# Moving the high parts of the key, value and output weights from ScalarE to GpSimd in the first pass of a gated cross-attention kernel

## The chip, the cores and the metric

The kernel runs on one core of a Trainium2 chip. The metric is the device time of one execution in microseconds (us), the median of several runs. The engines are named as the profile names them: PE is TensorE (matmuls), PEld its weight loads, DVE is VectorE, ACT is ScalarE, POOL is GpSimd and SP is SyncE, whose queue issues all the DMAs here.

## The reference

The block adds a gated cross-attention and then a gated quantised linear layer to `x` (32 sequences of 64 tokens, width 512). There are 32 query heads and 8 key/value heads of width 128.

```python
Q = (q @ Wq.T).reshape(b, s, HKV, exp, DK)      # q = layernorm(x)
K = (k @ Wk.T).reshape(b, s, HKV, DK)           # k = v = ctx
V = (v @ Wv.T).reshape(b, s, HKV, DV)
scores = jnp.einsum('bqhed,bkhd->bheqk', Q, K) * scale
scores = jnp.where(causal, scores, jnp.finfo(scores.dtype).min)
probs = jax.nn.softmax(scores, axis=-1)
attn = jnp.einsum('bheqk,bkhd->bqhed', probs, V)
attn @ Wd.T
...
x = x + jnp.tanh(g_xattn[0]) * _L0_xattn_ref(_layernorm(x), ctx, ctx, Wq, Wk, Wv, Wd)
x = x + jnp.tanh(g_ffn[0]) * _L0_ffn_ref(_layernorm(x), qweight, weight_scale, weight_zero_point, bias)
```

## The kernel before

**Numbers.** All is float32 in the reference. The kernel multiplies in float16: each operand is scaled by a power of two and split into a high part (the float16 value) and a low part (what is left, in float16), and a product is made of three matmuls: high by high, high by low, low by high (`PASSES`).

**Work.** The 2048 tokens are four blocks of 512, the heads are eight groups (one key/value head with its four query heads). A step `n` of the main loop is one group `g = n % 8` in one block `tb = n // 8`, so there are 32 steps. In step `n` PE makes the scores, the transposed probabilities, the products with the values (`av`) and, with the group's output weights `wd`, the four output tiles (`y_unit`, tile `py`), and between them, one step ahead, the queries, keys and values of step `m = n + 1` (tile `pa`). `y_unit(n, 0)` begins some 21 us into a step, and from there to the step's end nearly all of PE's work is `y_unit`.

**Weights.** The first eight steps (`tb == 0`) are the first pass. There the raw float32 weights of each group come from HBM and are scaled and split: `wq` by ACT (high part) and DVE (low part); `wk`, `wv` (one piece of 128x512 each per group) and `wd` (four pieces of 128x512) by ACT (high part, `split_wk`, `split_wv`, `split_wd` of ACT) and POOL (low part). For the low part POOL runs two instructions on a piece, `weight_lo`: `raw = raw * scale` in place (TENSOR_SCALAR, L430), then `lo = raw - high` (TENSOR_TENSOR, L432). The finished parts are written to HBM (`keep_qkv`, `keep_d`) and in later passes read back ready (`back_qkv`, `back_d`).

**Order.** Each engine has one queue, written by hand as a Python loop, and engines wait for each other by counting semaphores. In step `g` of the first pass POOL has: (in step 0 ahead of the rest, `wk(1)` and `wv(1)`), the twelve small instructions of `ln_rstd` where a layer norm falls due (step 6), the four pieces of `wd(g)`, the low parts of a normed block (`ln_lo`), two chunks of the next block's context (`ctx_lo`, steps 5 and 6), and `wk(g+2)`, `wv(g+2)` (steps 0 to 5). `wd` has a single buffer: `wd(g)` may be written only after the last `y_unit` of step `g-1` (`y_mm`) and after the copy to HBM of `wd(g-1)` (`d_kept`). The other weights have two buffers, by `g % 2`. The scale factors `w_mul` come from sums of squares (ACT), a small matmul (PE) and small DVE instructions (`weight_scale`), those for group `g+2` in step `g` just ahead of `y_unit(g, 0)`, after which PE waits for `wd_hi` and `wd_lo` (four counts per group).

**ACT's queue** in a step of the first pass, in short: `q_part 0`, `exp 0`, two pieces of `wd`, `q_part 1`, `p_part 0`, `exp 1`, two pieces of `wd`, `q_part 2`, squares of `wq(g+2)`, `p_part 1`, `q_part 3`, squares, `p_transposed 0`, squares of `wk` and `wv`, `k_part`, `p_transposed 1`, the `av` parts, `v_part`, `wq(g+2)`, `wk(g+2)`, `wv(g+2)`, squares of `wd`.

Of the kernel before, what the change touches and what calls it, by code (L numbers as in the profile page):

```python
# [52 lines left out]
def build(nc, x, ctxT, wqT, wkT, wvT, wdT, g_x, g_f, qw, w_scale, w_zero, bias, out):  # L53
    with ExitStack() as stack:
# [91 lines left out]
        q_kept, k_kept, v_kept, d_kept = sem("q_kept"), sem("k_kept"), sem("v_kept"), sem("d_kept")  # L146
# [111 lines left out]
        def _(sp):  # L258
# [25 lines left out]
            def keep_qkv(g):  # L284
# [120 lines left out]
        def _(pool):  # L405
# [117 lines left out]
        def _(act):  # L523
# [56 lines left out]
            def split_wk(g):  # L580
                act.wait_ge(w_mul_ok, scale_count(g, 1))
                wait(act, k_kept, 16 * (g - 1))
                act.wait_ge(wk_hi, g)
                act.activation(wk[:, g % 2, HI, :, :], raw_k[:, g % 2, :, :], ACT.Copy,
                               scale=w_mul[:, g, 1:2]).then_inc(wk_hi, 1)

            def split_wv(g):
                wait(act, v_kept, 16 * (g - 1))
# [857 lines left out]
```

## Time and profile before

| | |
|---|---|
| time, median of 3 runs | 1093.32 us (1093.08 to 1093.55) |
| profiled execution, its own time | 1090.95 us |
| its span, first to last instruction | 1089.2 us |
| busy: PE, DVE, ACT, POOL | 1033.6, 718.2, 489.3, 239.3 us |
| mean granted TensorE clock | 0.989 of full |

The span is what the trace covers; the profiled run's own time is 1.75 us longer, for what lies around it. A matmul's end is modelled in the trace, so PE's busy share tells that it is nearly always at work, not that each moment is full speed.

### The profile page before, as it was taken

Reading aid. Unit: us, or ns where it says so; the run is one execution under the profiler, and the core shown is the slowest. Engines: PE = TensorE matmul, PEld = TensorE weight load, DVE = VectorE, ACT = ScalarE, POOL = GpSimd, SP = SyncE. Lnnn points to the kernel's source line nnn. Section 1 sums busy time; section 2 is a strip of 40 time slices with the busy share of each in tenths; the row PEclk is TensorE's granted clock in tenths of the full one; section 3 lists DMA queues with packets and bytes.
Section 4 is the critical chain, followed back from the end, with each engine's and each line's share of the span. In section 5 each row is a group of like instructions: output and inputs, shape, how many; then the busy total and the mean of one; then the engine's idle time right before and its main releaser. Section 6 shows DMA issues by size and latency. Waiting matters only on the chain.

```text
span 1089.2 us, 20137 instructions
## 1 busy us (share of the span) xinstructions
PE 1033.6 (95%) x8000; PEld 582.6 (53%) x8000; DVE 718.2 (66%) x1347; ACT 489.3 (45%) x937; POOL 239.3 (22%) x242
## 2 busy tenths in 40 slices
PE   5899999999999999999999999999999999999974
PEld 3455554555555555555555555555555555555532
DVE  6856777677578566666665576755567566655567
ACT  5767675676534243353435334244434432333322
POOL 1545565466504100110004010110001300000012
PEclk9999999999999999999999999999999999999997
DMA  7647645435345133323332433332223233331101
GB/s 270 224 159 256 214 158 171 157 97 175 110 162 191 51 127 116 114 101 117 116 117 59 153 139 116 117 117 89 70 95 117 98 116 117 116 117 59 52 27 58
DMA packets 64250, 137.08 MB, mean 126 GB/s; under 512 B 5408, under 2 KB 38176, under 8 KB 53536
## 3 DMA queue, kind: packets, MB, share of 16 engines
q1 hardware_dynamic: 64160, 135.81, 36.4%
q8 instruction: 65, 1.06, 0.4%
q14 instruction: 25, 0.20, 0.1%
HBM read 93.85 MB, written 25.17 MB: 109 GB/s over the span
## 4 chain that ended last, share of the span: by engine, by line
PE 81%; DVE 8%; ACT 5%; issue 3%; POOL 0%; DVEq 0%; ACTq 0%; POOLq 0%
PE pa L1138 36%; PE py L1138 30%; PE av L1245 5%; PE ps L1212 3%; PE py L1295 3%; PE pp L1228 2%; PE av L1280 1%; DVE sc L846 1%; DVE row_max L850 1%; DVE sc L852 1%; ACT junk L542 1%; ACT junk L552 1%; DVE sc L863 1%; ACT pT L641 1%; DVE q L806 1%
## 5 line engine op out<-in xcount | busy, mean ns | idle before, releaser
L1138 PE MATMUL pa<-xT,wq 128*128 128x512 f16 x1536 | 347.1, 380 | 7.2 <-DVE q L806 4.6
L1138 PE MATMUL py<-wd,att 128*128 128x512 f16 x1536 | 349.8, 380 | 1.4 <-DVE att L876 1.3
L1138 PEld LDWEIGHTS pa<-xT,wq 128*128 128x128 f16 x1536 | 144.1, 98 | 179.6 <-issue 20.2
L1138 PEld LDWEIGHTS py<-wd,att 128*128 128x128 f16 x1536 | 148.9, 98 | 164.1 <-issue 4.0
L885 DVE SCALAR_TENSOR_TENSOR xacc<-py,f_y,xacc 128x512 f32<-128x512 f32 x128 | 96.0, 750 | 145.3 <-PE py L1138 145.3
L603 ACT ACTIVATE q<-pa 128x512 f16<-128x512 f32 x128 | 75.8, 592 | 235.2 <-PE pa L1138 235.1
L648 ACT ACTIVATE att<-av 128x256 f16<-128x256 f32 x256 | 80.9, 385 | 158.2 <-PE av L1245 157.8
L876 DVE SCALAR_TENSOR_TENSOR att<-av,att 128x256 f16<-128x256 f32 x256 | 93.6, 418 | 70.0 <-ACT att L648 70.0
L806 DVE SCALAR_TENSOR_TENSOR q<-pa,q 128x512 f16<-128x512 f32 x128 | 87.6, 685 | 22.6 <-ACT q L603 22.6
L1138 PE MATMUL pa<-wv,cT 128*128 128x128 f16 x1536 | 96.2, 219 | 0.0
L1138 PEld LDWEIGHTS pa<-wv,cT 128*128 128x128 f16 x1536 | 89.8, 98 | 0.9
L1138 PE MATMUL pa<-cT,wk 128*128 128x512 f16 x384 | 88.1, 379 | 0.8 <-DVE q L806 0.6
L1245 PE MATMUL av<-pT,v_dup 128*128 128x256 f16 x512 | 71.7, 273 | 6.4 <-ACT pT L641 6.4
L637 ACT CAST pr<-sc 128x512 f16<-128x512 f32 x64 | 39.6, 619 | 79.5 <-DVE sc L863 79.5
L486 POOL TENSOR_TENSOR xacc<-xacc,xn 128x512 f32<-128x512 f32 x12 | 15.2, 1268 | 265.8 <-DVE xacc L984 265.8
L806 DVE SCALAR_TENSOR_TENSOR k<-pa,k 128x512 f16<-128x512 f32 x32 | 22.1, 692 | 76.7 <-ACT k L608 76.7
L641 ACT COPY pT<-pp 128x1024 f16<-128x1024 f16 x64 | 64.4, 1006 | 4.8 <-PE pp L1228 4.8
L1245 PEld LDWEIGHTS av<-pT,v_dup 128*128 128x128 f16 x512 | 48.0, 98 | 26.3 <-ACT pT L641 7.6
L430 POOL TENSOR_SCALAR raw_d<-raw_d,w_mul 128x512 f32<-128x512 f32 x32 | 57.5, 1796 | 19.9 <-ACT wd L598 19.8
L1212 PEld LDWEIGHTS ps<-k,q 128*128 128x128 f16 x1536 | 53.2, 98 | 13.8 <-issue 0.9
L470 POOL TENSOR_TENSOR rs_t<-rs 128x4 f32<-128x4 f32 x18 | 3.9, 219 | 255.2 <-DVE rs L910 254.3
L1138 PEld LDWEIGHTS pa<-cT,wk 128*128 128x128 f16 x384 | 36.1, 98 | 40.5 <-issue 2.3
(112 smaller groups left out, 1115.3 us busy)
## 6 DMA issues: line engine op xcount, KB each, us to landing
wq<-kept_q SPq DMA_DIRECT2D x24, 1024.0 KB, 7.0
wd<-kept_d SPq DMA_DIRECT2D x24, 1024.0 KB, 4.8
v_dup<-v_nat SPq DMA_DIRECT2D x128, 128.0 KB, 2.4
raw_d<-in_wdT SPq DMA_DIRECT2D x8, 1024.0 KB, 8.8
kept_q<-wq SPq DMA_DIRECT2D x8, 1024.0 KB, 8.8
kept_d<-wd SPq DMA_DIRECT2D x8, 1024.0 KB, 4.8
raw_q<-in_wqT SPq DMA_DIRECT2D x7, 1024.0 KB, 5.5
wk<-kept_k SPq DMA_DIRECT2D x24, 256.0 KB, 7.4
```

What stands on the lines that cost most here:

```text
L430: pool.tensor_scalar(raw, raw, scale, None, ALU.mult).then_inc(w_scaled, 1)
L603: act.activation(q[:, HI, :, h, :], pa[h % 2][:, :].rearrange("p (b s) -> p b s", b=BPB), ACT.Copy, scale=Q_SCALE).then_inc(q_hi, 1)
L637: act.copy(pr[:, p, :, HI, :], sc[:, p, :, :]).then_inc(p_hi, 1)
L641: act.copy(pT[:, :, 2 * p:2 * p + 2, :], pp[:, :].bitcast(F16).rearrange("p (b e s) -> p b e s", b=BPB, e=2)).then_inc(pT_ok, 1)
L648: last = act.activation(att[:, HI, :, at:at + S], av[j % 2][:, bb * 256:(bb + 1) * 256].rearrange("p (h s) -> p h s", h=HPG), ACT.Copy, sc ...
L806: dve.scalar_tensor_tensor(out=out, in0=in0, scalar=scale, in1=hi, op0=ALU.mult, op1=ALU.subtract).then_inc(done, 1)
L876: last = dve.scalar_tensor_tensor(out=att[:, LO, :, at:at + S], in0=av[j % 2][:, bb * 256:(bb + 1) * 256].rearrange("p (h s) -> p h s", h= ...
L885: dve.scalar_tensor_tensor(out=acc(t), in0=py[j % 2][:, :], scalar=f_y[:, n:n + 1], in1=acc(t), op0=ALU.mult, op1=ALU.add).then_inc(y_ok, 1)
L1138: last = pe.matmul(out, stationary(a, i), moving(b, i), start=(i == 0 and (a, b) == PASSES[0]), stop=(i == count - 1 and (a, b) == PASSES[ ...
L1212: last = pe.matmul(ps[:, b * S:(b + 1) * S], q[:, a, b, 2 * p:2 * p + 2, :].rearrange("p e s -> p (e s)"), k[:, c, b * S:(b + 1) * S], sta ...
L1245: last = pe.matmul(av[j % 2][:, bb * 256:(bb + 1) * 256], v_dup[:, n % 2, b, c, :], pT[:, b, :, :].rearrange("p h s -> p (h s)"), start=(c ...
L1295: last = pe.matmul(py[t % 2][:, :], xT[:, par, a, i, t % TILES * P:(t % TILES + 1) * P], ff_w[:, i, :], start=(i == 0 and a == HI), stop=( ...
```

## The change

In the first pass, POOL makes the high part as well as the low part of `wk`, `wv` and `wd` (of `wk` and `wv` from group 1 on): a new TENSOR_SCALAR that reads the raw float32 piece and writes float16. ACT's six instructions per group for this are gone. POOL's queue takes over the waits that ACT had for them (the scale factors, the buffer free, the copy to HBM done), and the semaphores that count the copies of `wk` and `wv` to HBM become one per buffer. Everything else is in the same order.

```diff
-        q_kept, k_kept, v_kept, d_kept = sem("q_kept"), sem("k_kept"), sem("v_kept"), sem("d_kept")
+        q_kept, d_kept = sem("q_kept"), sem("d_kept")
+        k_kept, v_kept = pair("k_kept"), pair("v_kept")
...
-            def weight_lo(out, raw, hi, scale, done):
+            def weight_parts(hi, lo, raw, scale, hi_done, lo_done, parts):
 
                 nonlocal scaled
                 scaled += 1
+                pool.tensor_scalar(hi, raw, scale, None, ALU.mult).then_inc(hi_done, 1)
                 pool.tensor_scalar(raw, raw, scale, None, ALU.mult).then_inc(w_scaled, 1)
                 pool.wait_ge(w_scaled, scaled)
-                pool.tensor_tensor(out, raw, hi, ALU.subtract).then_inc(done, 1)
+                pool.wait_ge(hi_done, parts)
+                pool.tensor_tensor(lo, raw, hi, ALU.subtract).then_inc(lo_done, 1)
 
             def split_wd(g, h):
 
-                pool.wait_ge(wd_hi, 4 * g + h + 1)
+                if h == 0:
+                    pool.wait_ge(w_mul_ok, scale_count(g + 1, 3))
+                    wait(pool, y_mm, 4 * g)
+                    wait(pool, d_kept, 16 * g)
...
             def split_wk(g):
 
-                pool.wait_ge(wk_hi, g + 1)
+                pool.wait_ge(w_mul_ok, scale_count(g, 1))
+                wait(pool, k_mm, g - 1)
+                wait(pool, k_kept[g % 2], 16 * (g // 2))
+                pool.wait_ge(wk_hi, g)
                 pool.wait_ge(wk_lo, g)
...
-            def split_wd(g, h):
-                if h == 0:
-                    act.wait_ge(w_mul_ok, scale_count(g + 1, 3))
-                    wait(act, y_mm, 4 * g)
-                    wait(act, d_kept, 16 * g)
-                act.activation(wd[:, HI, h, :], raw_d[:, g % 2, h, :], ACT.Copy,
-                               scale=w_mul[:, g + 1, 3:4]).then_inc(wd_hi, 1)
...
                 exp(n, 0)
-                if tb == 0:
-                    split_wd(g, 0)
-                    split_wd(g, 1)
                 if ahead:
                     q_part(m, 1)
                 p_part(n, 0)
                 exp(n, 1)
-                if tb == 0:
-                    split_wd(g, 2)
-                    split_wd(g, 3)
```

POOL at the start of step 0, before (`wk`, `wv` of group 1, then the first piece of `wd(0)`):

```order
15 L430 TENSOR_SCALAR raw_k<-raw_k,w_mul 128x512 [waits wk_lo,wk_hi]
16 L432 TENSOR_TENSOR wk<-raw_k,wk 128x512 [waits w_scaled]
17 L430 TENSOR_SCALAR raw_v<-raw_v,w_mul 128x512 [waits wv_lo,wv_hi]
18 L432 TENSOR_TENSOR wv<-raw_v,wv 128x512 [waits w_scaled]
19 L430 TENSOR_SCALAR raw_d<-raw_d,w_mul 128x512 [waits wd_hi]
20 L432 TENSOR_TENSOR wd<-raw_d,wd 128x512 [waits w_scaled]
```

and in the change:

```order
15 L433 TENSOR_SCALAR wk<-raw_k,w_mul 128x512 [waits wk_lo,wk_hi,w_mul_ok]
16 L434 TENSOR_SCALAR raw_k<-raw_k,w_mul 128x512
17 L437 TENSOR_TENSOR wk<-raw_k,wk 128x512 [waits wk_hi,w_scaled]
18 L433 TENSOR_SCALAR wv<-raw_v,w_mul 128x512 [waits wv_lo,wv_hi]
19 L434 TENSOR_SCALAR raw_v<-raw_v,w_mul 128x512
20 L437 TENSOR_TENSOR wv<-raw_v,wv 128x512 [waits wv_hi,w_scaled]
21 L433 TENSOR_SCALAR wd<-raw_d,w_mul 128x512 [waits w_mul_ok]
22 L434 TENSOR_SCALAR raw_d<-raw_d,w_mul 128x512
23 L437 TENSOR_TENSOR wd<-raw_d,wd 128x512 [waits wd_hi,w_scaled]
```

A piece is three instructions in place of two, and the wait for ACT's high part is replaced by one for the scale factor.

POOL at the end of step 5 and the start of step 6, before (`wk(7)`, `wv(7)`, twelve instructions of `ln_rstd`, of which the first and the last stand here, then `wd(6)`):

```order
88 L430 TENSOR_SCALAR raw_k<-raw_k,w_mul 128x512 [waits wk_lo,wk_hi]
89 L432 TENSOR_TENSOR wk<-raw_k,wk 128x512 [waits w_scaled]
90 L430 TENSOR_SCALAR raw_v<-raw_v,w_mul 128x512 [waits wv_lo,wv_hi]
91 L432 TENSOR_TENSOR wv<-raw_v,wv 128x512 [waits w_scaled]
92 L470 TENSOR_TENSOR rs_t<-rs 128x4 [waits seed_ok]
...
103 L474 TENSOR_TENSOR rstd<-rs_t,rs 128x4 [waits rs_ok]
104 L430 TENSOR_SCALAR raw_d<-raw_d,w_mul 128x512 [waits wd_hi,rs_ok]
```

and in the change:

```order
124 L433 TENSOR_SCALAR wk<-raw_k,w_mul 128x512 [waits wk_hi,k_kept1,wk_lo,k_mm,w_mul_ok]
125 L434 TENSOR_SCALAR raw_k<-raw_k,w_mul 128x512
126 L437 TENSOR_TENSOR wk<-raw_k,wk 128x512 [waits wk_hi,w_scaled]
127 L433 TENSOR_SCALAR wv<-raw_v,w_mul 128x512 [waits wv_hi,wv_lo,v_kept1,v_mm]
128 L434 TENSOR_SCALAR raw_v<-raw_v,w_mul 128x512
129 L437 TENSOR_TENSOR wv<-raw_v,wv 128x512 [waits wv_hi,w_scaled]
130 L486 TENSOR_TENSOR rs_t<-rs 128x4 [waits seed_ok]
...
141 L490 TENSOR_TENSOR rstd<-rs_t,rs 128x4 [waits rs_ok]
142 L433 TENSOR_SCALAR wd<-raw_d,w_mul 128x512 [waits y_mm,d_kept,w_mul_ok,rs_ok]
```

The sequence is the same, with one more instruction per piece, and the first piece of `wd(6)` now waits for PE's last `y_unit` itself.

ACT in step 1, before, from the first `exp` to the squares of the query weights:

```order
69 L633 ACTIVATE sc<-sc 128x512 [waits shifted]
70 L598 ACTIVATE wd<-raw_d,w_mul 128x512 [waits d_kept,y_mm,w_mul_ok]
71 L598 ACTIVATE wd<-raw_d,w_mul 128x512
72 L603 ACTIVATE q<-pa 128x8x64 [waits q_mm]
73 L637 CAST pr<-sc 128x8x64 [waits norm_ok]
74 L633 ACTIVATE sc<-sc 128x512 [waits shifted]
75 L598 ACTIVATE wd<-raw_d,w_mul 128x512 x2
76 L603 ACTIVATE q<-pa 128x8x64 [waits q_mm]
77 L542 ACTIVATE junk,w_ss<-raw_q 128x1024 [waits w_ss_ok,wq_ld1]
```

and in the change:

```order
62 L628 ACTIVATE sc<-sc 128x512 [waits shifted]
63 L598 ACTIVATE q<-pa 128x8x64 [waits q_mm]
64 L632 CAST pr<-sc 128x8x64 [waits norm_ok]
65 L628 ACTIVATE sc<-sc 128x512 [waits shifted]
66 L598 ACTIVATE q<-pa 128x8x64 [waits q_mm]
67 L558 ACTIVATE junk,w_ss<-raw_q 128x1024 [waits w_ss_ok,wq_ld1]
```

Four instructions per step are gone here, and `wk`, `wv` at the step's end.

## Rows read from the trace of the kernel before

**Rows 1.** The page, part 1: busy us, share of span, instructions.

```profile
PE 1033.6 (95%) x8000; PEld 582.6 (53%) x8000; DVE 718.2 (66%) x1347; ACT 489.3 (45%) x937; POOL 239.3 (22%) x242
```

**Rows 2.** PE timeline, step 1: start us, duration us, what, idle before and its releaser.

```profile
92.14 0.61 PE L1228 MATMUL pp<-ident,pr 128*128 128x128 f16 x8 [0.29 <-ACT pT L641]
...
94.82 1.05 PE L1245 MATMUL av<-pT,v_dup 128*128 128x256 f16 x8 [0.73 <-ACT pT L641]
...
97.46 2.75 PE L1138 MATMUL py<-wd,att 128*128 128x512 f16 x12
```

**Rows 3.** Chain of waits, step 1: start us, us, what.

```profile
86.32 1.23 ACT wd L598 x2
...
89.06 0.51 ACT pr L637
```

**Rows 4.** DVE timeline, step 1, the softmax's last parts, and that step's scale factors.

```profile
83.98 1.15 DVE L863 SCALAR_TENSOR_TENSOR sc<-sc,row_inv 128x512 f32<-128x512 f32 x1
...
85.82 0.69 DVE L869 TENSOR_TENSOR pr<-sc,pr 128x512 f16<-128x512 f32 x1
...
87.38 0.98 DVE L863 SCALAR_TENSOR_TENSOR sc<-sc,row_inv 128x512 f32<-128x512 f32 x1
...
98.67 0.17 DVE L760 TENSOR_SCALAR w_mul<-w_exp 128x4 int32<-128x4 int32 x1
```

**Rows 5.** All instructions of a POOL line: duration ns min/median/max, first and last start.

```profile
L430 POOL TENSOR_SCALAR raw_d<-raw_d,w_mul x32: 1560/1997/2003, 47.4 to 291.7; 128x512 f32<-128x512 f32 x32
...
L486 POOL TENSOR_TENSOR xacc<-xacc,xn x12: 1262/1269/1272, 372.4 to 1063.3; 128x512 f32<-128x512 f32 x12
...
L421 POOL TENSOR_TENSOR cT<-c_raw,cT x14: 1155/1158/1229, 27.7 to 778.4; 128x512 f16<-128x512 f32 x14
```

**Rows 6.** POOL timeline, step 0: first and last piece.

```profile
41.23 1.57 POOL L430 TENSOR_SCALAR raw_k<-raw_k,w_mul 128x512 f32<-128x512 f32 x1 [11.11 <-ACT wk L584]
...
58.52 1.16 POOL L432 TENSOR_TENSOR wd<-raw_d,wd 128x512 f16<-128x512 f32 x1
```

**Rows 7.** DVE timeline, scale factors of group 1.

```profile
40.12 0.17 DVE L760 TENSOR_SCALAR w_mul<-w_exp 128x3 int32<-128x3 int32 x1
```

**Rows 8.** PE timeline, step 0: a wait, the first output tile, the last ones.

```profile
51.46 4.44 PE L1138 MATMUL pa<-xT,wq 128*128 128x512 f16 x12 [2.15 <-DVE q L806]
...
64.97 2.75 PE L1138 MATMUL py<-wd,att 128*128 128x512 f16 x12
...
71.02 5.34 PE L1138 MATMUL py<-wd,att 128*128 128x512 f16 x24
```

**Rows 9.** Busy time by stretch; behind the engines the granted clock, DMA share, GB/s.

```profile
51.40:56.00 4.60, 4.54 (x17) 1.90 (x18) 3.76 (x6) 3.83 (x8) 4.43 (x4) 0.63 0.97 371
```

**Rows 10.** POOL timeline, step 1: a piece of the output weights.

```profile
81.78 1.57 POOL L430 TENSOR_SCALAR raw_d<-raw_d,w_mul 128x512 f32<-128x512 f32 x1 [2.77 <-ACT wd L598]
83.43 1.16 POOL L432 TENSOR_TENSOR wd<-raw_d,wd 128x512 f16<-128x512 f32 x1
84.56 2.00 POOL L430 TENSOR_SCALAR raw_d<-raw_d,w_mul 128x512 f32<-128x512 f32 x1
```

**Rows 11.** POOL timeline, end of step 5 and step 6.

```profile
232.60 2.38 POOL L421 TENSOR_TENSOR cT<-c_raw,cT 128x512 f16<-128x512 f32 x2 [5.04 <-ACT c_raw L570]
238.54 2.09 POOL L430 TENSOR_SCALAR raw_k<-raw_k,w_mul 128x512 f32<-128x512 f32 x1 [3.55 <-ACT wk L584]
...
245.38 0.20 POOL L470 TENSOR_TENSOR rs_t<-rs 128x4 f32<-128x4 f32 x1
...
249.15 2.00 POOL L430 TENSOR_SCALAR raw_d<-raw_d,w_mul 128x512 f32<-128x512 f32 x1
...
260.46 1.16 POOL L432 TENSOR_TENSOR wd<-raw_d,wd 128x512 f16<-128x512 f32 x1
```

**Rows 12.** PE timeline: last output tiles of step 5, first of step 6.

```profile
236.97 5.34 PE L1138 MATMUL py<-wd,att 128*128 128x512 f16 x24
...
262.25 2.75 PE L1138 MATMUL py<-wd,att 128*128 128x512 f16 x12
```

More of the change, by code:

```diff
@@ L424, in _ @@
             scaled = 0
-            def weight_lo(out, raw, hi, scale, done):
+            def weight_parts(hi, lo, raw, scale, hi_done, lo_done, parts):
                 nonlocal scaled
                 scaled += 1
+                pool.tensor_scalar(hi, raw, scale, None, ALU.mult).then_inc(hi_done, 1)
                 pool.tensor_scalar(raw, raw, scale, None, ALU.mult).then_inc(w_scaled, 1)
                 pool.wait_ge(w_scaled, scaled)
-                pool.tensor_tensor(out, raw, hi, ALU.subtract).then_inc(done, 1)
+                pool.wait_ge(hi_done, parts)
+                pool.tensor_tensor(lo, raw, hi, ALU.subtract).then_inc(lo_done, 1)
             def split_wd(g, h):
-                pool.wait_ge(wd_hi, 4 * g + h + 1)
-                weight_lo(wd[:, LO, h, :], raw_d[:, g % 2, h, :], wd[:, HI, h, :], w_mul[:, g + 1, 3:4], wd_lo)
+                if h == 0:
+                    pool.wait_ge(w_mul_ok, scale_count(g + 1, 3))
+                    wait(pool, y_mm, 4 * g)
+                    wait(pool, d_kept, 16 * g)
+                weight_parts(wd[:, HI, h, :], wd[:, LO, h, :], raw_d[:, g % 2, h, :], w_mul[:, g + 1, 3:4],
+                             wd_hi, wd_lo, 4 * g + h + 1)
             def split_wk(g):
-                pool.wait_ge(wk_hi, g + 1)
+                pool.wait_ge(w_mul_ok, scale_count(g, 1))
+                wait(pool, k_mm, g - 1)
+                wait(pool, k_kept[g % 2], 16 * (g // 2))
+                pool.wait_ge(wk_hi, g)
                 pool.wait_ge(wk_lo, g)
-                weight_lo(wk[:, g % 2, LO, :, :], raw_k[:, g % 2, :, :], wk[:, g % 2, HI, :, :], w_mul[:, g, 1:2], wk_lo)
+                weight_parts(wk[:, g % 2, HI, :, :], wk[:, g % 2, LO, :, :], raw_k[:, g % 2, :, :], w_mul[:, g, 1:2],
+                             wk_hi, wk_lo, g + 1)
             def split_wv(g):
-                pool.wait_ge(wv_hi, g + 1)
+                wait(pool, v_mm, g - 1)
+                wait(pool, v_kept[g % 2], 16 * (g // 2))
+                pool.wait_ge(wv_hi, g)
                 pool.wait_ge(wv_lo, g)
-                weight_lo(wv[:, g % 2, LO, :, :], raw_v[:, g % 2, :, :], wv[:, g % 2, HI, :, :], w_mul[:, g, 2:3], wv_lo)
+                weight_parts(wv[:, g % 2, HI, :, :], wv[:, g % 2, LO, :, :], raw_v[:, g % 2, :, :], w_mul[:, g, 2:3],
+                             wv_hi, wv_lo, g + 1)
             def ln_lo(t):
@@ L578, in split_wq @@
                                scale=w_mul[:, g, 0:1]).then_inc(wq_hi, 1)
[L580 to L588, printed above, removed]
-                act.wait_ge(wv_hi, g)
-                act.activation(wv[:, g % 2, HI, :, :], raw_v[:, g % 2, :, :], ACT.Copy,
-                               scale=w_mul[:, g, 2:3]).then_inc(wv_hi, 1)
-            def split_wd(g, h):
-                if h == 0:
-                    act.wait_ge(w_mul_ok, scale_count(g + 1, 3))
-                    wait(act, y_mm, 4 * g)
-                    wait(act, d_kept, 16 * g)
-                act.activation(wd[:, HI, h, :], raw_d[:, g % 2, h, :], ACT.Copy,
-                               scale=w_mul[:, g + 1, 3:4]).then_inc(wd_hi, 1)
             def q_part(m, h):
@@ L686, in _ @@
                         split_wq(1, h)
-                    split_wk(1)
-                    split_wv(1)
                 if ahead:
```

13 lines of the change are left out of this document (6 added, 7 removed).

## The prediction

> **What bounds the kernel now.** I read the page first: PE is busy for 1033.6 us of the 1089.2 us span, ACT, DVE and POOL are far from full [rows 1]. So whatever makes PE wait is lost, and whatever fills a wait of PE is won. Then I read PE's own timeline, step by step. In a usual step of the first pass (1 to 5) PE stops twice for ACT's copy of the transposed probabilities, 0.29 and 0.73 us, 1.02 us in all, before it begins its output tiles 32.49 us after those of the step before (64.97 and 97.46) [rows 2, 8]. That is all that relief for ACT can win in such a step. Last I read POOL's timeline against the start of PE's output tiles, since PE waits there for both parts of `wd`. In step 0 POOL ends `wd(0)` at 59.68 us and PE begins at 64.97 us: 5.3 us to spare [rows 6, 8]. In step 6 POOL ends `wd(6)` at 261.62 us and PE begins at 262.25 us: 0.6 us to spare [rows 11, 12]. The share of 22% for POOL hides this; it is an average over four passes, three of which have no weights to split.
>
> **What one new instruction costs.** No row shows a TENSOR_SCALAR of POOL with float16 output. The nearest is the one on the same raw piece with float32 output: 1.56 us at least, 2.00 us where it collides with DVE [rows 5]. On TENSOR_TENSOR a float16 output is cheaper than a float32 one by 0.11 us (1.158 against 1.269) [rows 5]. That gives 1.45 us alone; with a share of the collisions (0.44 us each, about one in three) I take **1.6 us**, and 1.3 to 2.0 us as bounds. The lower bound is no row's, it lets the float16 store save twice what it saves on TENSOR_TENSOR.
>
> The Trainium skill says in "GPSIMD Engine Reference", section 4.1 (Engine selection), that GpSimd runs one-input elementwise work at roughly line rate and only two-input work about twice as slow as VectorE. The trace disagrees: its one-input TENSOR_SCALAR takes 1.56 us where its two-input TENSOR_TENSOR takes 1.16 us [rows 5, 10]. If the rule held for the new form, there would be no late `wd`; that is a rival below.
>
> **Step 0: a loss.** POOL's six pieces took from 41.23 to 59.68 us, 18.45 us [rows 6]. They can now start when the scale factors are there (40.29 us, plus 0.1 us as latency, as between other engines) and not after ACT's high part: 0.8 us sooner [rows 7]. Six new instructions add 9.6 us: 40.4 + 18.45 + 9.6 = 68.45 us, against 64.97 us for PE's first output tile [rows 8]. **PE waits 3.5 us** (1.7 to 5.9 us by the bounds). Nothing is late behind it that would hide it: PE's output tiles are the next thing in its queue. POOL is not held further, as `wk(2)`, `wv(2)` follow, whose factors are known before that and whose 10 us end before PE's last tile of the step (76.36 us [rows 8], plus the delay).
>
> **The clock after such a wait.** After PE's wait of 2.15 us at 51.46 us, twelve matmuls take 4.44 us in place of the 2.75 us of the same dozen elsewhere [rows 2, 8], and the granted clock in that stretch is 0.63 of full [rows 9]: it fell to 1.2 GHz for a part of it. So a wait of 3.5 us should cost another 1.7 us. I add it, and keep 0 as the lower bound: short waits of 0.7 us show none.
>
> **Steps 1 to 5: does POOL keep up?** Its turn for `wd` begins when PE has ended the last tile of the step before (76.36 us for step 1 [rows 8]); until now it began at 81.78 us, after ACT's high part [rows 10]. The block of four pieces took 12.47 us (249.15 to 261.62 [rows 11]); with 4 x 1.6 us it takes 18.9 us and ends at 95.3 us, against PE's 97.46 us [rows 2]: no wait. `wk` and `wv` may begin at 98.84 us [rows 4], took 6.84 us (238.54 to 245.38 [rows 11]) and now 10.0 us: 108.9 us, just when PE ends step 1 (76.36 + 32.49 = 108.85 us). With 2.0 us for an instruction it runs 0.9 us over and PE waits 0.1 us. So POOL, which before waited 2.77 us for ACT even between `wv` and `wd` [rows 10], has no room left, but PE pays nothing. The new waits of POOL (`y_mm`, `d_kept`, `w_mul_ok`, the copies) hold nothing else: behind them in its queue stand only the next weights. SP's `keep_d` and `load_d` leave about 1 us later, at the end of `wd`; the squares that read `raw_d` are ACT's last work of a step, and ahead of its next work, which needs PE's first queries of the next step. I cost that at nothing; if that cover were gone, it would be the 1 us of a step by which the load is late.
>
> **Steps 1 to 5: what ACT's relief wins.** Of its six instructions per step, the pair of `wd` ahead of `q_part 2` lies on the chain (1.23 us) [rows 3]; the others lie in ACT's waits or behind its critical part. Without it ACT reaches its second `pr` up to 1.23 us earlier than 89.06 us [rows 3], but that needs DVE's normalised scores, which end at 87.38 + 0.98 = 88.36 us [rows 4]. So it wins about 0.6 us, half of PE's 1.02 us, and DVE is late next. From this I take off 0.2 us: DVE and POOL get in each other's way more often. What the rows show of that: L863 takes 1.15 us in place of its 0.69, since it starts inside POOL's TENSOR_TENSOR (83.43 to 84.59); the TENSOR_SCALAR that follows is stretched from 1.57 to 2.00 us; but L869, which starts in the middle of that TENSOR_SCALAR, takes the plain 0.69 us [rows 4, 10]. So a TENSOR_TENSOR holds DVE up, a TENSOR_SCALAR hardly does after its start. The number of TENSOR_TENSORs stays, only their places move. I take **0.4 us a step, 2.0 us for five**; bounds: 5 us won (all of 1.02 us), 2.5 us lost (each step catches one more collision on its chain than now).
>
> **Step 6: a loss.** POOL comes out of `ctx_lo` at 234.98 us and waited 3.55 us for ACT's `wk` [rows 11]; that wait is gone. `wk(7)`, `wv(7)` take 6.84 + 3.2 = 10.0 us: 245.0 us, where before it was 245.38 us. So here the gain of the earlier start is used up. `ln_rstd` takes 3.77 us (245.38 to 249.15): 248.8 us. `wd(6)` takes 18.9 us: **267.7 us against 262.25 us** [rows 12]. PE waits 5.4 us (3.6 to 7.8 us by the bounds), plus 1.7 us of slow clock. Before, ACT made the high part of `wd(6)` while POOL was at `ln_rstd`, so the wait for it cost POOL nothing there. Step 7 has no `wk`, `wv` and no `ln_rstd` ahead of `wd(7)`: free. After the first pass the kernels are the same.
>
> **The sum.** 3.5 + 1.7 (step 0) - 2.0 (steps 1 to 5) + 5.4 + 1.7 (step 6) = +10.3 us. On the profiled execution's own time of 1090.95 us (span 1089.2) that is 1101.3 us; that run lies 2.4 us under the median of the three, 1093.32 us, against which I predict: **1103.6 us**.
>
> **Rivals.**
> 1. *The new instruction is cheap* (faster). If it took 0.6 us, POOL would be done at 62.5 us in step 0, before 64.97. In step 6 it would end at 234.98 + 8.04 + 3.77 + 14.87 = 261.7 us, before 262.25. No wait is left, and the relief for ACT stays: 2 to 5 us won, about 1090 us. It decides for itself below some 0.9 us, where the waits (none and 1.2 us) drop under the gain. For it speaks only that no row shows this form; against it, that the same operation on the same input takes 1.56 us [rows 5]. This is also what the page's line rate would give.
> 2. *Collisions with DVE on the critical chain.* POOL now works through nearly all of the step. If each of steps 1 to 5 catches one more collision of 0.46 us (1.15 against 0.69 us [rows 4]) and wins nothing else, they lose 2.3 us in place of winning 2.0, and POOL's own pieces stretch to the 2.0 us bound: (5.9 + 1.7) + 2.3 + (7.8 + 1.7) = +19.4 us, 1113 us; half of that stretch gives 1109 us.
> 3. *A POOL instruction locks DVE out for its whole length.* Then every two-input instruction of DVE would wait on average half of 1.6 us; four of them lie on a step's chain (both L852, both L863): 3 us a step, 15 us for five, 1121 us with the sum above. L869's plain 0.69 us speaks against it [rows 4]. The Trainium skill has this rule in "SBUF — State Buffer", section "SBUF: two separate sides": the shared pair is an exclusive lock held for the whole instruction. By the row it isn't so for TENSOR_SCALAR.
> 4. *Waits without a slow clock*: as forecast, less 3.4 us: 1100.2 us. It lies within the forecast's range.
>
> **How the numbers follow.** Forecast, with rival 4 in it: 0.72 (1097 to 1109 us). Rival 1: 0.10. Rival 2: 0.12. Rival 3: 0.03. Another 0.03 for a time within noise, where small waits and gains cancel. The range of 80% is 1096.5 to 1111 us: it has the forecast's case and most of rival 2 and leaves out rivals 1 and 3. A measurement of this kernel tells about 0.2% (2.2 us) from no change: faster than 1091.1 us 0.09, between 0.06, slower than 1095.5 us 0.85.
>
> **What would show it.** In the trace of the changed kernel: POOL's new TENSOR_SCALAR at 1.45 to 2.0 us; PE's first output tile of steps 0 and 6 with an idle time of 3 to 6 us before it, released by POOL's `wd`; behind it a dozen matmuls of 4.4 us; in steps 1 to 5 no wait for `wd`, and 0.3 to 0.7 us less wait for the transposed probabilities; ACT's busy time down by 46 instructions, some 28 us at half of 1.23 us each, POOL's up by 46 x 1.6 = 74 us. The forecast is wrong if the new instruction takes under 1 us, if POOL's time stretches the DVE chain by over a microsecond a step, or if PE's wait in step 6 is made up later, for which I see no place.

## The result and the profile after

The changed kernel took **1102.5 us** (median of four runs, 1101.27 to 1103.47) beside 1093.2 us (1092.28 to 1093.55) for the kernel before on the same chip: a ratio of **1.0086, 95% interval 1.0068 to 1.0103**. It is slower by 9.4 us; 1103.6 us was predicted. Its profiled execution spans 1100.8 us against 1089.2, with a mean clock of 0.984 against 0.989.

The page of the changed kernel, part 1 (busy us, share of span, instructions), answers to [rows 1]; the second line is the start of part 4, the share of each engine in the chain that ended last:

```profile
PE 1036.2 (94%) x8000; PEld 584.2 (53%) x8000; DVE 720.6 (65%) x1347; ACT 462.3 (42%) x891; POOL 308.2 (28%) x288
...
PE 79%; DVE 8%; POOL 5%; ACT 4%; issue 4%; DMA 1%; SPq 0%; DVEq 0%; POOLq 0%; ACTq 0%
```

ACT has 27.0 us and 46 instructions less, POOL 68.9 us and 46 instructions more. POOL is busy for only 28% of the span and yet now has 5% of the chain, some 55 us: nearly all of it lies in two steps.

PE timeline, step 0 and step 6 of the changed kernel (start us, duration us, what, idle before and its releaser); the `py` rows answer to [rows 8, 12]:

```profile
68.72 5.16 PE L1122 MATMUL py<-wd,att 128*128 128x512 f16 x12 [4.99 <-issue]
...
251.06 0.86 PE L1196 MATMUL ps<-k,q 128*128 128x64 f16 x24 [0.67 <-ACT q L598]
...
271.25 4.44 PE L1122 MATMUL py<-wd,att 128*128 128x512 f16 x12 [3.51 <-issue]
```

The profile names no releaser here ("issue"). POOL's timeline names it: its last pieces of those two steps end at 68.62 and 271.15 us, 0.1 us before PE goes on.

```profile
67.47 1.15 POOL L437 TENSOR_TENSOR wd<-raw_d,wd 128x512 f16<-128x512 f32 x1
...
270.00 1.15 POOL L437 TENSOR_TENSOR wd<-raw_d,wd 128x512 f16<-128x512 f32 x1
```

Behind both waits the dozen matmuls that takes 2.75 us elsewhere takes 5.16 and 4.44 us. Busy time by stretch, changed kernel; the clock is the third number from the end, as in [rows 9]:

```profile
68.70:73.90 5.20, 5.18 (x14) 1.96 (x15) 0.00 (x0) 0.00 (x0) 5.12 (x4) 0.53 0.87 262
271.20:275.80 4.60, 4.55 (x15) 1.88 (x16) 0.07 (x1) 0.00 (x0) 0.00 (x0) 0.63 0.84 269
```

It was granted near 1.2 GHz (0.5 of full) for all or most of these stretches.

**Where the time went.** I compared the starts of the steps (the first score matmul of each) in both traces:

| | before, us | after, us | difference |
|---|---|---|---|
| start of step 0 | 39.39 | 40.27 | +0.88 |
| length of step 0 | 36.80 | 42.09 | +5.29 |
| steps 1 and 2 | 32.50 each | 31.48 each | -1.02 each |
| steps 3, 4, 5 | 35.95, 32.51, 32.50 | 36.17, 32.73, 32.73 | +0.22, +0.22, +0.23 |
| step 6 | 33.91 | 39.79 | +5.88 |
| step 7 | 31.71 | 31.34 | -0.37 |
| steps 8 to 30 | 723.13 | 722.94 | -0.19 |
| start of step 31 to the end | 58.3 | 59.8 | +1.5 |

The first pass (steps 0 to 7) carries the loss: 5.29 - 1.37 + 5.88 - 0.37 = +9.4 us, where 1.37 us is the sum over steps 1 to 5. The 0.88 us ahead of step 0 lie where the two kernels are alike, and the 1.5 us at the end come from a slow stretch of the clock that sits elsewhere; the experiments' traces vary by as much in both places. Steps 1 to 5 won 1.0 us each or lost 0.2 us, and I had not expected two kinds of them.

### The profile page after: what moved, and what is told of

Its sections match the earlier page's. It is cut to its first block, busy times and chain, and to the rows that moved or that the text cites. A ratio compares the mean times of both kernels' runs of the same rounds, so it can differ in the third digit from the quotient of the medians.

```text
span 1100.8 us, 20182 instructions
## 1 busy us (share of the span) xinstructions
PE 1036.2 (94%) x8000; PEld 584.2 (53%) x8000; DVE 720.6 (65%) x1347; ACT 462.3 (42%) x891; POOL 308.2 (28%) x288
## 4 chain that ended last, share of the span: by engine, by line
PE 79%; DVE 8%; POOL 5%; ACT 4%; issue 4%; DMA 1%; SPq 0%; DVEq 0%; POOLq 0%; ACTq 0%
PE pa L1122 35%; PE py L1122 30%; PE av L1229 5%; PE ps L1196 3%; PE py L1279 2%; PE pp L1212 2%; PE av L1264 1%; POOL wd L433 1%; DVE sc L836 1%; DVE sc L847 1%; POOL raw_d L434 1%; DVE sc L830 1%; DVE row_max L834 1%; ACT junk L568 1%; DVE row_sum L843 1%
## 5 line engine op out<-in xcount | busy, mean ns | idle before, releaser
L1122 PE MATMUL py<-wd,att 128*128 128x512 f16 x1536 | 356.0, 385 | 9.4 <-issue 8.5
L433 POOL TENSOR_SCALAR wd<-raw_d,w_mul 128x512 f16<-128x512 f32 x32 | 57.0, 1780 | 11.0 <-issue 10.9
```

What stands on the lines that cost most here:

```text
L433: pool.tensor_scalar(hi, raw, scale, None, ALU.mult).then_inc(hi_done, 1)
L1122: last = pe.matmul(out, stationary(a, i), moving(b, i), start=(i == 0 and (a, b) == PASSES[0]), stop=(i == count - 1 and (a, b) == PASSES[ ...
```

## The experiments

Each ratio is to the kernel before on the same chip; three sets of runs, in which that kernel took 1091.79, 1091.91 and 1091.39 us.

### One part of the change at a time

**e1_kv_only**: ACT keeps the high parts of `wd`; POOL makes those of `wk` and `wv`.

```diff
                 exp(n, 0)
+                if tb == 0 and g < GROUPS:
+                    split_wd(g, 0)
+                    split_wd(g, 1)
...
                 exp(n, 1)
+                if tb == 0 and g < GROUPS:
+                    split_wd(g, 2)
+                    split_wd(g, 3)
```

> The change for the key and value weights alone: GpSimd makes their high parts, ScalarE keeps those of wd. Theory (two late wd blocks make the loss): in step 0 GpSimd has 2 instead of 6 new instructions of 1.48 us, ends wd(0) some 6 us sooner than in the changed kernel and ahead of PE; in step 6 the 3.0 us of new work are paid by the 3.55 us that it no longer waits for ScalarE. No wait of PE for wd, and ScalarE's two instructions lie off the chain: 1093 us, within 1.5 us. Rival (any added GpSimd work slows VectorE's chain, and that is the loss): a third of the change's new work, so about a third of its 9.3 us: 1096 us.

Measured: 1093.11 us, ratio 1.0009 (0.9992 to 1.0026). PE waits nowhere for `wd`, and steps 1 to 5 have the waits of [rows 2] unchanged. PE timeline, step 1:

```profile
91.07 0.61 PE L1238 MATMUL pp<-ident,pr 128*128 128x128 f16 x8 [0.29 <-ACT pT L656]
...
93.74 1.05 PE L1255 MATMUL av<-pT,v_dup 128*128 128x256 f16 x8 [0.73 <-ACT pT L656]
...
96.39 2.75 PE L1148 MATMUL py<-wd,att 128*128 128x512 f16 x12
```

So `wk` and `wv` alone neither cost nor win anything in steps 1 to 5. Step 6 of this trace is 1.1 us longer than before (35.00 against 33.91 us; the point on step 6 below tells what part of it is). The interval of the ratio has room for that 1.1 us as well as for nothing.

**e2_wd_only**: the reverse, ACT makes the high parts of `wk` and `wv`, POOL those of `wd`.

```diff
+                    split_wk(1)
+                    split_wv(1)
                 if ahead:
                     q_part(m, 0)
...
                 av_part(n, 3)
+                if prep:
+                    split_wk(g + 2)
+                    split_wv(g + 2)
```

> The change for the output weights alone: ScalarE keeps the high parts of the key and value weights. Theory: step 0 ends wd(0) at about 41.2 + 18.45 + 4 x 1.48 = 65.6 us, 0.6 us over the 64.97 us of before, plus 2 us of slow clock if PE's wait is long enough; step 6 is late as in the changed kernel (+5.9 us), since GpSimd still waits for ScalarE's wk; steps 1 to 5 lose up to 0.5 us each because wd begins later, or win up to 1 us: 1098 to 1101 us, with PE's wait for wd in step 6 of 3 to 4.5 us. Rival (the loss needs all six new instructions): under 1096 us.

Measured: 1098.73 us, ratio 1.0068 (1.0045 to 1.0091). PE timeline, steps 0 and 6:

```profile
64.92 4.17 PE L1141 MATMUL py<-wd,att 128*128 128x512 f16 x12 [1.68 <-issue]
...
266.45 4.93 PE L1141 MATMUL py<-wd,att 128*128 128x512 f16 x12 [5.06 <-issue]
```

`wd` alone makes most of the loss. In step 0 the wait is 3.3 us shorter than in the whole change: POOL has two new instructions less ahead of `wd(0)` and is done 2.6 us sooner, counted from the start of the step, and PE comes 0.7 us later. In step 6 the wait is longer, as POOL waits for ACT's `wk(7)` again.

Steps 1, 2, 4 and 5 take 32.33 to 32.35 us here, a win of 0.15 to 0.17 us, so the 1.0 us of the whole change is not the sum of its parts (none from `wk` and `wv`, 0.17 us from `wd`). POOL begins `wd` later, behind the `wk` and `wv` that waited for ACT, and its first TENSOR_TENSOR on `wd` then meets DVE's second shift of the scores. DVE and POOL timelines, step 1:

```profile
84.06 1.46 DVE L855 TENSOR_TENSOR sc<-sc,row_max 128x512 f32<-128x512 f32 x1
...
83.82 1.16 POOL L437 TENSOR_TENSOR wd<-raw_d,wd 128x512 f16<-128x512 f32 x1
```

That shift takes 0.69 us in the kernel before and in step 1 of the whole change, where it starts inside a TENSOR_SCALAR of POOL.

**e7_pairs_alone**: the kernel before with only its counting changed.

```diff
-        q_kept, k_kept, v_kept, d_kept = sem("q_kept"), sem("k_kept"), sem("v_kept"), sem("d_kept")
+        q_kept, d_kept = sem("q_kept"), sem("d_kept")
+        k_kept, v_kept = pair("k_kept"), pair("v_kept")
...
-                wait(act, k_kept, 16 * (g - 1))
+                wait(act, k_kept[g % 2], 16 * (g // 2))
```

> The kernel before with only the second part of the change: the copies of wk and wv to HBM counted by buffer, ScalarE still makes all high parts. Theory: the copies are long done when they are waited for, so nothing moves: ratio to before 1.000, within 0.15%. Rival (ScalarE or SyncE waits less or more for the copies): a difference over 2 us.

Measured: 1092.92 us, ratio 1.0006 (0.9992 to 1.002). Nothing.

### The two late blocks

**e3_act_0_6**: the whole change, but ACT makes the high parts of `wd` in steps 0 and 6.

```diff
                 exp(n, 0)
+                if tb == 0 and g in (0, 6):
+                    split_wd(g, 0)
+                    split_wd(g, 1)
...
                 exp(n, 1)
+                if tb == 0 and g in (0, 6):
+                    split_wd(g, 2)
+                    split_wd(g, 3)
```

> The changed kernel, but in steps 0 and 6 ScalarE makes the high parts of wd as before. Theory: both waits of PE for wd go, with them +5.3 and +5.9 us; what is left of the changed kernel's difference is steps 1 to 5 (-1.0, -1.0, +0.2, +0.2, +0.2 us): 1102.5 - 11 = 1091.5 us, 1090 to 1093. Rival (steps 1 to 5 pay by contention what they win): the two waits go but the time comes out at 1094 to 1097 us.

Measured: 1088.40 us, ratio **0.9972 (0.9959 to 0.9986)**: faster than both kernels, and 1.6 us under the bottom of what I expected. PE timeline, the first output tiles of steps 0 and 6:

```profile
65.50 2.75 PE L1148 MATMUL py<-wd,att 128*128 128x512 f16 x12
...
258.32 2.75 PE L1148 MATMUL py<-wd,att 128*128 128x512 f16 x12
```

Both waits and both slow dozens are gone, and with them 12.4 us by the ratios (1.0086 - 0.9972, of 1092 us). By the traces step 0 is 5.8 us and step 6 4.8 us shorter than in the changed kernel, 10.6 us in sum: the two blocks carry the whole loss. Steps 1 to 5 are another 4.2 us shorter, for four of them now took 31.48 us and only step 3 the longer form, without the slow dozen that stands in step 3 of the changed kernel (more on both below). Step 6 is still 1.1 us longer than before.

**e4_fill**: the whole change, PE multiplies by the identity while it would wait.

```diff
+FILL = {0: 20, 6: 13}
...
                 if j == 0:
+                    if n in FILL:
+                        wait(pe, y_ok, 4 * n)
+                        for _ in range(FILL[n]):
+                            pe.matmul(py[0][:, :], ident[:, :], ident[:, :].unsqueeze(1).to_broadcast([P, BT // P, P]),
+                                      start=True, stop=True)
                     if n < GROUPS:
                         pe.wait_ge(wd_hi, 4 * (n + 1))
```

> The changed kernel with matmuls on the identity, whose result nobody reads, in PE's queue ahead of its wait for wd: 20 of 512 columns in step 0 (4.3 us of the 4.99 us wait), 13 in step 6 (2.8 us of 3.51). PE waits as long as before but is at work meanwhile. Theory (the slow matmuls behind the waits come from PE's idle time): the granted clock stays full there, the first dozen of output matmuls takes 2.75 us in place of 5.16 and 4.44, and the kernel is 4.1 us faster than the changed one: 1098.4 us. Rival (the slow dozen has another cause, such as the DMA traffic of that moment): 1102.5 us as the changed kernel, or a bit more.

Measured: 1096.79 us, ratio 1.0051 (1.0033 to 1.0068), 3.8 us less than the changed kernel by the ratios. PE timeline, steps 0 and 6:

```profile
64.06 4.48 PE L1240 MATMUL py<-ident 128*128 128x512 f16 x20
68.38 2.75 PE L1123 MATMUL py<-wd,att 128*128 128x512 f16 x12
...
260.67 2.97 PE L1240 MATMUL py<-ident 128*128 128x512 f16 x13
264.33 2.75 PE L1123 MATMUL py<-wd,att 128*128 128x512 f16 x12 [0.70 <-issue]
```

PE goes on no sooner than the late weights allow (in step 0 even 0.9 us after POOL's last piece, since the filling is a little too long), but the dozen behind is at full speed. So the second term, the slow clock, is real, and it goes with PE's idleness and not with the late weights. The filling is no cure, only a probe.

### What steps 1 to 5 win, and what takes it back

**e10_act_relief**: the kernel before, ACT makes only one column of the pieces 3 and 4 of `wd` in steps 1 to 5. The rest of those high parts is left out; POOL's work is as before.

```diff
-                act.activation(wd[:, HI, h, :], raw_d[:, g % 2, h, :], ACT.Copy,
+                some = slice(0, 1) if 0 < g < 6 and h >= 2 else slice(0, D)
+                act.activation(wd[:, HI, h, some], raw_d[:, g % 2, h, some], ACT.Copy,
                                scale=w_mul[:, g + 1, 3:4]).then_inc(wd_hi, 1)
```

> The kernel before, but in steps 1 to 5 ScalarE converts only one column of the third and fourth piece of wd (the high parts of those pieces are left out), so that its pair ahead of q_part 2 costs some 0.3 us less than 1.23 us and all of GpSimd's work stays where it was. It measures ScalarE's relief by itself. Theory (as in the prediction): VectorE's normalised scores are late next, and its 0.46 us collision with GpSimd stays, so PE's wait for the transposed probabilities shrinks by 0.3 to 0.6 us a step, the 0.35 us wait for the queries stays: 2 to 3 us under before, ratio 0.9975. Rival (relief of ScalarE alone gives the 1.0 us a step seen in the changed kernel's first steps): 5 us under before, ratio 0.9955.

Measured: 1089.82 us, ratio 0.9981 (0.9970 to 0.9991). The pair with one column takes 0.47 us in the trace, in place of 1.23 us. A step takes 31.92 to 31.93 us in place of 32.50, so ACT's relief by itself wins **0.57 us**. PE timeline, step 1:

```profile
87.25 2.75 PE L1139 MATMUL pa<-xT,wq 128*128 128x512 f16 x12 [0.34 <-DVE q L807]
...
95.63 1.05 PE L1246 MATMUL av<-pT,v_dup 128*128 128x256 f16 x8 [0.62 <-ACT pT L642]
```

Of the two waits for the transposed probabilities one is gone and one left with 0.62 us. The 0.34 us for DVE's `q` stays, because DVE's first normalise still takes 1.15 us as in [rows 4]. ACT's second `pr` now waits for DVE, whose second normalise ends at 89.73 us, so DVE is late next, as forecast. ACT timeline, step 1:

```profile
89.76 0.62 ACT L638 CAST pr<-sc 128x512 f16<-128x512 f32 x1 [0.18 <-DVE sc L864]
```

In the changed kernel's steps 1 and 2 that first normalise (L847) takes 0.69 us, 0.46 us less, which fits the rest of the 1.02 us. In steps 3 to 5 something else happens. DVE timeline of the changed kernel, the first shift of the scores (L836) and the first normalise, in step 1 and in step 3:

```profile
85.88 0.69 DVE L836 TENSOR_TENSOR sc<-sc,row_max 128x512 f32<-128x512 f32 x1
...
90.15 0.69 DVE L847 SCALAR_TENSOR_TENSOR sc<-sc,row_inv 128x512 f32<-128x512 f32 x1
...
148.84 1.70 DVE L836 TENSOR_TENSOR sc<-sc,row_max 128x512 f32<-128x512 f32 x1
...
154.11 1.18 DVE L847 SCALAR_TENSOR_TENSOR sc<-sc,row_inv 128x512 f32<-128x512 f32 x1
```

and POOL's timeline at the same two moments:

```profile
85.88 1.71 POOL L437 TENSOR_TENSOR wd<-raw_d,wd 128x512 f16<-128x512 f32 x1
...
148.83 1.16 POOL L437 TENSOR_TENSOR wd<-raw_d,wd 128x512 f16<-128x512 f32 x1
```

Both engines start a two-input instruction within 0.01 us of each other, since both were released by the end of the step before. One of them then takes its own time (0.69 or 1.16 us) and the other 0.55 to 1.0 us more. When DVE is the one held, PE waits for it (step 3, changed kernel; step 1 has no wait here):

```profile
156.03 2.75 PE L1122 MATMUL pa<-xT,wq 128*128 128x512 f16 x12 [1.38 <-DVE q L790]
```

Two kernels test whether that start decides the step. **e8_pool_later** is e3_act_0_6 with POOL a little later, **e9_dve_later** the same with DVE a little later.

```diff
                     wait(pool, y_mm, 4 * g)
                     wait(pool, d_kept, 16 * g)
+                    pool.memset(nudge[:, :], 0.0)
```

> The kernel with ScalarE's high parts in steps 0 and 6, plus one tiny GpSimd memset (about 0.1 us) ahead of the wd pieces in steps 1 to 5 and 7. In the traces GpSimd's first subtraction and VectorE's first two-input instruction of a step start within 0.01 us of each other, and who comes first changes from step to step: 0.69 us for VectorE's and 1.71 us for GpSimd's, or 1.70 and 1.16. Theory (a tie for the shared port, worth 1.25 us a step when GpSimd wins): 0.1 us later GpSimd loses always, all five of VectorE's instructions take 0.69 us, every step 1 to 5 is 1.0 us shorter than before, and the time is 1 to 4 us under the kernel without the memset (which was 0.9972 of before): 0.993 to 0.9965 of before. Rival (no tie, the long ones come from elsewhere): some 1.70 us instructions remain and the time is unchanged, 0.997.

```diff
+                if tb == 0 and 0 < g < 6:
+                    dve.tensor_scalar(nudge[:, :], ones[:, :], 1.0, None, ALU.mult)
                 scores(n, 0)
```

> The same kernel (ScalarE's high parts in steps 0 and 6) without the memset, but with one tiny VectorE instruction (128x1, about 0.1 us) ahead of the scores in steps 1 to 5. Theory (tie for the port): now GpSimd is first always, VectorE's first two-input instruction takes about 1.6 us in all five steps, each of them ends 0.2 to 0.3 us later than before instead of 1.0 us earlier: 2 to 5 us over the kernel without the tiny instruction, 0.999 to 1.002 of before. Rival: only the 0.1 us each, 0.5 us in all, 0.9975.

Measured: e8_pool_later 1087.82 us, ratio **0.9961 (0.9948 to 0.9974)**; e9_dve_later 1093.37 us, ratio 1.0019 (1.0007 to 1.0030). An instruction of 0.10 us on POOL or 0.15 us on DVE decides over 1.25 us a step: DVE's first shift takes 0.69 us in all five steps of e8_pool_later and 1.64 us in all five of e9_dve_later. That e8_pool_later is faster than e3_act_0_6 (0.9961 against 0.9972) can't be told, since the intervals overlap. Step 1 of e8_pool_later, POOL's timeline:

```profile
79.75 1.69 POOL L438 TENSOR_TENSOR wd<-raw_d,wd 128x512 f16<-128x512 f32 x1
```

and DVE's, where the shift (L864) is the first by 0.02 us:

```profile
79.73 0.69 DVE L864 TENSOR_TENSOR sc<-sc,row_max 128x512 f32<-128x512 f32 x1
```

Step 1 of e9_dve_later, POOL's timeline:

```profile
79.44 1.16 POOL L438 TENSOR_TENSOR wd<-raw_d,wd 128x512 f16<-128x512 f32 x1
```

and DVE's, where shift and normalise both are held:

```profile
79.50 1.64 DVE L863 TENSOR_TENSOR sc<-sc,row_max 128x512 f32<-128x512 f32 x1
...
84.72 1.18 DVE L874 SCALAR_TENSOR_TENSOR sc<-sc,row_inv 128x512 f32<-128x512 f32 x1
```

Step lengths: 31.47 us in steps 1, 2, 4 and 5 of e8_pool_later, 32.72 to 32.74 us in those of e9_dve_later. In step 3 (34.91 and 34.47 us) a slow dozen in e8_pool_later hides the difference.

**e11_after_nudged**: POOL's tiny instruction in the whole change (diff as for e8_pool_later).

> The changed kernel whole, with one tiny POOL instruction (a memset of one column) ahead of the first piece of the output weights of every step, so that DVE's first shift is no longer level with POOL's first TENSOR_TENSOR. Theory: in steps 3, 4 and 5 DVE's shift of the scores drops from 1.70 to 0.69 us and those steps are 31.47 us long in place of 32.73, as in the kernel with ACT's help in steps 0 and 6; steps 1 and 2 stay as they are. That is 3 x 1.25 = 3.8 us less than the changed kernel (ratio 1.0086): 1.0052 (1.004 to 1.0065). The late output weights of steps 0 and 6 stay: PE waits 4 to 6 us in both, since each block is 0.1 us longer and PE is there sooner in step 6. Rival: what steps 3 to 5 win, PE only loses again before the output weights of step 6, since that wait is set by POOL's own queue, which starts step 6's pieces from the context work of step 5: if POOL's queue is bound from step 3 on, the time stays at 1.0086.

Measured: 1100.48 us, ratio 1.0082 (1.0068 to 1.0096). The steps did what the theory said: 31.48 us for steps 1, 2, 4 and 5 and 33.23 us for step 3. The time did not: 0.4 us less than the change by the ratios, not 3.8. In its profiled execution the eight steps of the first pass are 3.8 us shorter than in the changed kernel's, the whole span only 2.3 us (1098.5 against 1100.8). The slow clock took back some of what the ties gave. Behind the wait of step 6 it lasted longer (PE timeline):

```profile
266.67 5.28 PE L1124 MATMUL py<-wd,att 128*128 128x512 f16 x12 [3.53 <-issue]
271.74 1.06 PE L1231 MATMUL av<-pT,v_dup 128*128 128x256 f16 x4
```

These are 1.3 us more than the 4.44 and 0.60 us of the changed kernel after a wait of nearly the same length (3.51 us). The rival named POOL's queue; that did not bind, as the wait of step 6 is unchanged. The medians as they stand are 2.0 us apart, on two chips, and the intervals of the two ratios allow any gain from none to some 3 us. The mean granted clock was 0.981 in all four timed runs of e11_after_nudged and 0.980 to 0.984 in those of the changed kernel, which leans to the clock as the taker and doesn't show it. How much the timed runs gain, and why it is less than 3.8 us, is not settled.

### The clock in step 3

Where the context's norm is made, PE waits 1.18 us in step 3. Behind it stands a dozen matmuls of 4.2 to 4.4 us in six traces (before, after, e1_kv_only, e7_pairs_alone, e8_pool_later, e10_act_relief) and of 2.75 us in five (e2_wd_only, e3_act_0_6, e4_fill, e9_dve_later, e11_after_nudged). **e12_best_filled** is e8_pool_later with that wait filled.

```diff
                 pe.wait_ge(c_ss_ok, 2 * tb + 2)
+                if tb == 1:
+                    wait(pe, y_ok, 12)
+                    for _ in range(5):
+                        pe.matmul(py[0][:, :], ident[:, :], ident[:, :].unsqueeze(1).to_broadcast([P, BT // P, P]),
+                                  start=True, stop=True)
                 pe.wait_ge(w_exp_ok, w_before)
```

> The fastest version so far (ACT makes the high parts of the output weights in steps 0 and 6, the tiny POOL instruction ahead of them in the others; ratio 0.9961, and a dozen matmuls of 4.21 us behind PE's wait of 1.18 us in step 3), with five more matmuls of 128x512 by the identity (some 1.15 us) put into that wait of step 3. They write a tile that the next output tile starts afresh. Theory that the clock falls there because PE has nothing to do: no slow dozen in step 3 (2.75 us), the wait shrinks to under 0.2 us, and the time is 1.5 us less: 0.9948 (0.9938 to 0.996). Rival, since in other runs the same wait of 1.18 us was followed by 2.75 us: the clock falls there for another reason (what PE did before, or a limit in time), and a slow dozen stands in step 3 or soon after it in spite of the filling: 0.9961 or a little more.

Measured: 1086.14 us, ratio 0.9956 (0.9942 to 0.9970). PE timeline of e12_best_filled, step 3:

```profile
159.91 1.24 PE L1324 MATMUL py<-ident 128*128 128x512 f16 x5
161.14 0.60 PE L1314 MATMUL pp<-c_ss,ones 128*128 128x1 f32 x4
161.60 2.75 PE L1150 MATMUL py<-wd,att 128*128 128x512 f16 x12
```

and of e8_pool_later, without the filling:

```profile
160.71 0.58 PE L1314 MATMUL pp<-c_ss,ones 128*128 128x1 f32 x4 [1.18 <-DVE w_exp L769]
161.15 4.21 PE L1150 MATMUL py<-wd,att 128*128 128x512 f16 x12
```

Step 3 is 1.75 us shorter (33.16 against 34.91 us), as the theory of PE's idleness wants it. The mean granted clock leans the same way: 0.988 or 0.989 in all four timed runs of e12_best_filled, 0.984 to 0.989 in the six of e8_pool_later. But five kernels that fill nothing there had no slow dozen in step 3 either, and the ratios of e8_pool_later and e12_best_filled overlap. So it fits and isn't shown. e12_best_filled has the lowest median of all, 1086.14 us; that it is faster than e8_pool_later can't be told.

## Why the prediction was right, point by point

- **What bounds the kernel** held: POOL's share of the span said nothing, its slack against PE's first output tile of steps 0 and 6 said all. e3_act_0_6 shows it: without the two late blocks the change is a gain of 0.3%.
- **The new instruction**: all 46 take 1.55 us at least and 2.0 us when they collide with DVE. My 1.45 us for one alone was too low. It came from two TENSOR_TENSOR forms of 1.16 and 1.27 us [rows 5] that I took to differ by their output alone; they differ in their second input too (float16 in the first, float32 in the second), so those 0.11 us can't be put down to the output. The value I worked with, 1.6 us, was too high all the same. `wd(6)` took 17.78 us (253.37 to 271.15) against 12.47 before, so 1.33 us for each new instruction; the six pieces of step 0 took 27.35 us against 18.45, 1.48 us each. The reason is in POOL's timeline. Before, the raw TENSOR_SCALAR behind a TENSOR_TENSOR was often stretched to 2.00 us [rows 10]; now the new instruction stands there and is stretched in its place. In these two blocks the stretched ones are no more than before (three and three in step 0, one against three in step 6), so the new instruction brings its own 1.56 us and takes some off its neighbour.
- **Step 0** was right in sum by luck: +5.29 us against 3.5 + 1.7 = 5.2. Both terms were too small. The block was 0.7 us shorter than forecast, yet PE waited 4.99 us, and the dozen behind the wait cost 2.4 us. What I had not forecast pays for that: PE came 2.1 us sooner (63.73 less the 0.88 us of later start, against 64.97), and 4.99 + 2.4 - 2.1 = 5.3. Of the 2.1 us, 1.7 are the slow dozen at 51.46 us [rows 8], which was not there this time. It isn't the change that took it away: behind the same wait of 2.0 to 2.15 us it stands in seven traces, e1_kv_only, e3_act_0_6 and e4_fill among them, and is missing in four.
- **Step 6**: +5.88 us against 7.1. The mis-sized term is POOL's work from `ctx_lo` to the last piece of `wd(6)`: 31.4 us (239.75 to 271.15) against 10.0 + 3.8 + 18.9 = 32.7. The wait was 3.51 us for 5.4, the clock +1.69 us as said. PE's wait was shorter also because PE came 0.7 us later than forecast: it stopped 0.67 us before its second scores, at 251.06 us. The profile names ACT's `q` there, but the kernel's wait at that place is for DVE's masked scores (L830), and these were late since DVE's `wq` was held up by POOL's last TENSOR_TENSOR of `wv(7)`, which now runs at that moment. DVE timeline, then POOL's, changed kernel:

```profile
248.18 1.59 DVE L790 SCALAR_TENSOR_TENSOR wq<-raw_q,w_mul,wq 128x512 f16<-128x512 f32 x1
...
250.17 0.75 DVE L830 SCALAR_TENSOR_TENSOR sc<-ps,f_score,mask 128x512 f32<-128x512 f32 x1
...
248.07 1.15 POOL L437 TENSOR_TENSOR wv<-raw_v,wv 128x512 f16<-128x512 f32 x1
```

  That `wq` took 0.74 us before. In the whole change the 0.67 us cost nothing, as PE would have waited for `wd(6)` that much longer. With e1_kv_only and e3_act_0_6, where `wd(6)` is in time, they are part of the 1.1 us by which step 6 is longer than before. So my sentence that the earlier start of `wk(7)` and `wv(7)` just uses itself up missed a cost.
- **Steps 1 to 5, POOL**: it kept up, as forecast. In step 1 `wd` was done at 101.05 us, 1.6 us before PE's 102.61 us, and `wv(3)` at 113.87 us, with PE's step ending at 113.84 us. (With 2.0 us for an instruction my numbers give 0.8 us over and a wait of 0.2 us, not 0.9 and 0.1.)
- **Steps 1 to 5, ACT and DVE**: -1.4 us against -2.0. ACT's relief was right to 0.03 us (0.57 measured alone, 0.6 forecast). The step that failed is "I take off 0.2 us": collisions are not a small mean. They decide between a win of 1.02 us and a loss of 0.22 us by who starts first. That the win equals the 1.02 us of PE's two waits is chance: one of these waits stays with 0.62 us, and a collision less on DVE makes up for it, so 1.02 us was not the bound that I called it. Rival 2, one more collision on DVE's chain in a step, came true in three of five steps, at 1.25 us and not 0.46: the shift collides as well as the normalise. (By its own terms, half of rival 2's stretch gives 17.0 us and 1110 us, not 1109.)
- **Rival 1** (cheap instruction) fell at 1.55 us. **Rival 3** (a lock of full length for every two-input instruction of DVE) fell for TENSOR_SCALAR. In step 1 the first normalise starts at 90.15 us, inside POOL's TENSOR_SCALAR that runs from 89.12 to 90.71 us, and takes its plain 0.69 us. For TENSOR_TENSOR the measured hold of 0.95 to 1.01 us, where DVE starts within 0.06 us of a POOL instruction of 1.16 us, is close to the rule of the Trainium skill, "SBUF — State Buffer", section "SBUF: two separate sides". **Rival 4** (no slow clock) fell: the two slow dozens cost 2.4 and 1.7 us, and in e4_fill both are gone and the time is 3.8 us less.
- That the waits that moved to POOL, the DMAs behind them and the separate counting cost nothing is borne out by e7_pairs_alone and, within its interval, e1_kv_only, which take the time of the kernel before, and by steps 7 to 30.

What I left on the table was in the same numbers. The late blocks were known by step, so leaving just these two to ACT was the better change: 0.9972 of the time before with e3_act_0_6, 0.9961 with e8_pool_later.

## What to carry to other kernels

Price new work on a lightly used engine in the step where its deadline is tightest, not by its share of the span: here 28% busy was late twice, by 5.0 and 3.5 us, and the other steps had room. A shift of work need not be all or nothing; the two steps without slack can stay as they were. Where DVE and POOL are released by the same event and then both touch SBUF with two inputs, the order of their first instructions is worth fixing on purpose.

## What was unexpected in the hardware

- On POOL the one-input TENSOR_SCALAR (128x512) takes 1.56 us with float16 as with float32 output, while the two-input TENSOR_TENSOR takes 1.16 us (float16 out, second input float16) and 1.27 us (float32 out, second input float32, [rows 5]). POOL timeline of the changed kernel, step 1:

```profile
82.69 1.56 POOL L433 TENSOR_SCALAR wd<-raw_d,w_mul 128x512 f16<-128x512 f32 x1 [5.21 <-issue]
84.23 1.56 POOL L434 TENSOR_SCALAR raw_d<-raw_d,w_mul 128x512 f32<-128x512 f32 x1
```

- When DVE starts a two-input instruction inside a TENSOR_TENSOR of POOL, it is held for what is left of POOL's, less some 0.15 us: with 1.10, 0.92 and 0.61 us left (e9_dve_later, e2_wd_only, [rows 4, 10]) it took 0.95, 0.77 and 0.46 us more than its plain 0.69 us. Inside a TENSOR_SCALAR of POOL it took the plain 0.69 us.
- A tie of 0.01 us between DVE and POOL falls one way or the other from step to step of the same execution, and is worth 1.25 us of PE's time each time here.
- After a wait of PE of 3.5 us the slow clock cost 1.7 us in one trace and 3.0 us in another (3.51 and 3.53 us). After 1.18 us it came in some traces and not in others. I take from it that a forecast of this kernel can't be much finer than a microsecond or two.
